# Latent cross attention: keys folded into the ranks of head pairs, scores in two 64-row tiles

## The reference, cut to what matters

```python
q_hk = (hidden_q @ Wq.T).reshape(b, s, H, K)            # H = 16, K = 128
q_big = einsum('bshk,hkq->bshq', q_hk, w_kc_q)          # 384 wide
# layer 2 only: q_big is rotated with sin and cos of the position
kv_rope = kv_c * cos + rotate_half(kv_c) * sin          # (8, 361, 128), shared by all heads
q_r = einsum('bshq,hqr->bhsr', q_big, W_qr)             # 64 ranks per head
k_r = einsum('bld,hdr->bhlr', kv_rope, W_kr)            # 64 ranks per head
scores = einsum('bhsr,bhlr->bhsl', q_r, k_r)
attn = softmax(scores)
ctx_c = einsum('bhsl,bld->bhsd', attn, kv_rope)
ctx_lat = einsum('bhsd,hkd->bshk', ctx_c, w_kc_kv)
out = ctx_lat.reshape(b, s, H * K) @ Wo.T
```

## Time and profile before

| | |
|---|---|
| median of 3 runs | 3009.69 us (3003.22 to 3016.32) |
| profiled execution | span 3002.4 us on the device; its own time is not given beside the span |
| TensorE matmul busy | 2860.6 us, 95% |
| VectorE / ScalarE / GpSimd busy | 1385.1 / 1012.4 / 554.0 us |
| `mscores` matmuls (L1284) | 512 records (2 per fp32 matmul), 166.7 us busy |

### The profile page before, as it was taken

How to read it: one execution, slowest core, us unless ns; L and a number is a source line. 1 busy time by engine, 2 the same in 40 slices (tenths; PEclk the granted TensorE clock), 3 DMA queues, 4 the chain that set the end, 5 groups by cost and what they waited for, 6 DMA issues and landing times.

```text
span 3002.4 us, 37287 instructions
## 1 busy us (share of the span) xinstructions
PE 2860.6 (95%) x14562; PEld 1792.8 (60%) x14562; DVE 1385.1 (46%) x2699; ACT 1012.4 (34%) x2950; POOL 554.0 (18%) x518
## 2 busy tenths in 40 slices
PE   8999988999899999999899899999999988999998
PEld 4555554555666665678655455555554555777767
DVE  4410364511755556611246667676446767111115
ACT  2310172100633334322154222323214473444431
POOL 0000030000110000034112222121000031777750
PEclk9999999999889999999999999999999998999998
DMA  4011102100001110268400000001000102896566
GB/s 176 28 42 49 56 29 84 51 32 0 1 32 67 49 52 29 78 218 297 131 18 24 27 15 35 28 22 60 28 22 29 53 23 73 298 332 203 186 179 156
DMA packets 66675, 249.09 MB, mean 83 GB/s; under 512 B 26554, under 2 KB 28602, under 8 KB 53764
## 3 DMA queue, kind: packets, MB, share of 16 engines
q1 hardware_dynamic: 31776, 177.88, 17.3%
q0 software_dynamic: 31344, 65.30, 6.4%
q10 hardware_dynamic: 3380, 3.53, 0.4%
HBM read 274.53 MB, written 42.13 MB: 105 GB/s over the span
## 4 chain that ended last, share of the span: by engine, by line
PE 80%; DVE 10%; ACT 6%; DMA 2%; issue 1%; POOL 1%; SPq 0%; ACTq 0%; POOLq 0%; DVEq 0%
PE P L1030 32%; PE P L1034 13%; PE P L1416 10%; PE P L1040 4%; PE P L1302 4%; PE P L1284 4%; ACT A L1563 4%; PE P L1059 2%; PE P L1042 1%; DMA A<-outputs 1%; PE P L1275 1%; DVE A L2057 1%; DVE A L2055 1%; DVE A L2056 1%; PE P L1265 1%; PE P L1045 1%
## 5 line engine op out<-in xcount | busy, mean ns | idle before, releaser
L1030 PE MATMUL P<-A,W 128*128 128x400 f32 x1680 | 610.1, 502 | 5.4 <-DVE A L1981 2.9
L1030 PEld LDWEIGHTS P<-A,W 128*128 128x128 f32 x1680 | 317.4, 191 | 245.1 <-issue 7.0
L1476 ACT ACTIVATE A<-P 128x400 f32<-128x400 f32 (+6 forms) x535 | 279.1, 535 | 531.4 <-PE P L1302 170.8
L1030 PE MATMUL P<-X,W 128*128 128x400 f32 x816 | 307.2, 514 | 11.0 <-DMA W<-weights 8.2
L2394 POOL TENSOR_TENSOR A<-A,small 100x1600 f32<-100x1600 f32 x32 | 91.6, 2862 | 1070.1 <-DVE small L1921 1070.1
L2333 DVE TENSOR_TENSOR A<-P,A 128x128 f32<-128x128 f32 (+1 forms) x141 | 44.9, 318 | 457.0 <-ACT A L1729 457.0
L1030 PEld LDWEIGHTS P<-X,W 128*128 128x128 f32 x816 | 155.6, 194 | 130.2 <-issue 17.9
L1563 ACT ACTIVATE A<-A,small 100x100 f32<-100x100 f32 (+1 forms) x640 | 227.5, 366 | 2.2 <-DVE small L1916 2.2
L1040 PE MATMUL P<-C,A 128*128 128x128 f32 (+5 forms) x1511 | 209.8, 261 | 16.7 <-DVE A L1961 5.0
L1040 PEld LDWEIGHTS P<-C,A 128*128 128x128 f32 (+5 forms) x1511 | 168.7, 141 | 65.7 <-issue 38.2
L1034 PE MATMUL P<-A,W 128*128 128x400 f32 x496 | 207.0, 499 | 0.0
(11 more groups left out here) (287 smaller groups left out, 4283.7 us busy)
## 6 DMA issues: line engine op xcount, KB each, us to landing
W<-weights SPq DMA_DIRECT2D x60, 1024.0 KB, 4.8
A<-experts SPq DMA_DIRECT2D x16, 1536.0 KB, 7.7
W<-experts SPq DMA_DIRECT2D x28, 768.0 KB, 5.4
KT<-experts SPq DMA_DIRECT2D x15, 768.0 KB, 6.0
W<-weights SPq DMA_DIRECT2D x17, 640.0 KB, 3.9
A<-experts SPq DMA_DIRECT2D x14, 768.0 KB, 5.6
A<-outputs SPq DMA_DIRECT2D x12, 768.0 KB
W<-outputs SPq DMA_DIRECT2D x8, 768.0 KB
```

The costliest lines, as they stand in the source:

```text
L1030: self.e.matmul(out, a, b, start=i == 0, stop=False)
L1476: self.e.activation(out, in_, ACT.Copy).then_inc(*self.of(*item))
```

## The change

Instead of bringing each query out of its 64 ranks to width 128 (`keyed`), the keys are brought into the ranks. A new step `mkeys` computes, for a group and a batch, the keys of two head pairs: `WK` (128 x 128, the `W_kr` of two heads side by side) times `kf`, 128 x 361 per pair. ScalarE copies them to `KH`, two buffers. `mkeys` of batch t + 1 stands directly behind `mscores` of batch t; the first stands ahead of the loop. `mscores` now multiplies `QR` rows 64a to 64a + 63 with the same rows of `KH`: two heads per pair in two 64-row tiles, and all four banks are taken ahead of the first. `keyed` and `QE` go away, `QR` holds four pairs, and `W_kr` comes by a load of its own per layer (`key_ranks`, 512 KB) instead of with each pair's piece. Some semaphores are shared between kinds of events of the same engine.

```diff
+    def mkeys(self, c, g, b):                              # TensorE
+        self.wait_ge(self.at("key_ranks", c.n))
+        self.wait_ge(self.at("kf", b))
+        for i in range(2):
+            P = self.take(("fold", "kh", c.n, g, b, i), ("kh", c.n, g, b, i))
+            self.e.matmul(P[:, 0:L], c.WK[:, 2 * g + i, :], self.k.kf[:, b, :], start=True,
+                          stop=True).then_inc(*self.of("fold", "kh", c.n, g, b, i))
...
-    def keyed(self, c, p, half):                           # TensorE
-        piece = self.k.load(c.pre, "h", p)
-        P = [self.take(("fold", "qe", c.n, 2 * p + a, half), ("qe", c.n, 2 * p + a, half)) for a in range(2)]
-        self.wait_ge(self.at("qr", c.n, p, half))
-        for a in range(2):
-            rows = slice(64 * a, 64 * a + 64)
-            self.e.matmul(P[a][:, 0:H2], self.k.slot(piece)[rows, 1152:1280], c.QR[rows, p % 2, hs(half)],
-                          start=True, stop=True).then_inc(*self.of("fold", "qe", c.n, 2 * p + a, half))
...
     def mscores(self, c, g, b):
-        for i in range(4):
-            P = self.take(("scores", c.n, g, b, i), ("mexp", c.n, g, b, i))
-            self.wait_ge(self.at("qe", c.n, 4 * g + i, b // 4))
-            self.wait_ge(self.at("kf", b))
-            self.e.matmul(P[0:S, 0:L], c.QE[g % 2][:, i, ss(b)], self.k.kf[:, b, :],
-                          start=True, stop=True).then_inc(*self.of("scores", c.n, g, b, i))
+        P = [self.take(("scores", c.n, g, b, i), ("mexp", c.n, g, b, i)) for i in range(4)]
+        for p in range(2):
+            self.wait_ge(self.at("qr", c.n, 2 * g + p, b // 4))
+            self.wait_ge(self.at("kh", c.n, g, b, p))
+            for a in range(2):
+                rows, i = slice(64 * a, 64 * a + 64), 2 * p + a
+                self.e.matmul(P[i][0:S, 0:L], c.QR[rows, (2 * g + p) % 4, ss(b)], c.KH[rows, b % 2, p, :],
+                              start=True, stop=True).then_inc(*self.of("scores", c.n, g, b, i))
...
+    def mkeys(self, c, g, b):                              # ScalarE
+        self.wait_ge(self.at("x", c.n - 1, 1))
+        if 8 * g + b >= 2:
+            self.wait_ge(self.at("scores", c.n, (8 * g + b - 2) // 8, (b - 2) % 8, 3))
+        for i in range(2):
+            self.wait_ge(self.at("fold", "kh", c.n, g, b, i))
+            self.copy(c.KH[:, b % 2, i, :], self.ps("fold", "kh", c.n, g, b, i)[:, 0:L], "kh", c.n, g, b, i)
...
         yield from (s for s in tail if s)
+        yield "mkeys", c, 0, 0
         for g in range(4):
...
                 if t < NB:
                     yield "mscores", c, g, t
+                if t + 1 < NB:
+                    yield "mkeys", c, g, t + 1
+                elif t == NB and g < 3:
+                    yield "mkeys", c, g + 1, 0
                 yield from steps[n:]
...
-                    more = {1: q[:2], 2: [b[0], q[2]], 3: [b[1], q[3]], 4: [f[0], b[2], k[0], q[4]], 5: [b[3], q[5]],
-                            6: [f[1], b[4], k[1], q[6]], 7: [b[5], q[7]], 8: [f[2], b[6], k[2]], 9: [b[7]]}
+                    more = {1: q[:2], 2: [b[0], q[2]], 3: [b[1], q[3]], 4: [f[0], b[2], q[4]], 5: [b[3], q[5]],
+                            6: [f[1], b[4], q[6]], 7: [b[5], q[7]], 8: [f[2], b[6]], 9: [b[7]]}
...
+            for i, pre in enumerate(("L1_attn_", "L2_attn_")):    # SyncE
+                if p.index >= RING and k.loads[p.index - RING].name == (pre, "o"):
+                    self.wait_ge(self.at(*k.loads[p.index - RING].free))
+                    self.dma("key_ranks", k.subs[4 + 3 * i].WK.rearrange("p h r -> p (h r)"), k.KR[i], "key_ranks", 4 + 3 * i)
             self.piece(p, wd)
```

More of the change, by code:

```diff
@@ L17 @@
 FIRST = 127
+SHARED = {"crossing": "crossed", "up_scale": "scale", "wd_scale": "scale", "weighed": "averaged",
+          "token_of": "list", "tokens": "list", "indices": "list", "ends": "list", "rows": "list",
+          "tiles_of": "places", "end": "places", "slot_of": "places", "ended": "places", "slots": "places"}
 def fm(w):
@@ L769, in plain @@
             first = [(name, c, p) for name in ("mfold", "efold") for p in pairs]
-            query, keyed = ([(name, c, p, half) for half in range(2) for p in pairs] for name in ("query", "keyed"))
-            return first + query[:2] + keyed[:2] + query[2:] + keyed[2:]
+            query = [("query", c, p, half) for half in range(2) for p in pairs]
+            return first + query
         def units(g):
@@ L777, in units @@
             q, b = ([(name, c, 2 * p + a, half) for p, half in pairs for a in range(2)] for name in ("query", "big"))
-            f, k = ([(name, c, p, half) for p, half in pairs] for name in ("fold", "keyed"))
-            return q, b, f, k
+            f = [("fold", c, p, half) for p, half in pairs]
+            return q, b, f
         def back(g, half):
@@ L820, in mla @@
             ahead = plain(0)
-            ahead, left = ahead[:8], ahead[8:]
+            ahead, left = ahead[:6], ahead[6:]
         for step in ahead:
@@ L1229, in mfold @@
         i.then_inc(*self.of("fold", "m", c.n, p))
+        piece.free = "fold", "m", c.n, p
     def efold(self, c, p):
@@ L1627, in fold @@
         self.wait_ge(self.at("fold", "qr", c.n, p, half))
-        self.copy(c.QR[:, p % 2, hs(half)], self.ps("fold", "qr", c.n, p, half)[:, 0:H2], "qr", c.n, p, half)
-    def keyed(self, c, p, half):
-        for h in (2 * p, 2 * p + 1) if c.roped else (2 * p,):
-            self.wait_ge(self.at("fold", "qe", c.n, h, half))
-            self.copy(c.QE[(h // 4) % 2][:, h % 4, hs(half)], self.ps("fold", "qe", c.n, h, half)[:, 0:H2], "qe", c.n, h, half)
+        self.copy(c.QR[:, p % 4, hs(half)], self.ps("fold", "qr", c.n, p, half)[:, 0:H2], "qr", c.n, p, half)
+    def mkeys(self, c, g, b):
[5 more added lines that the diff above has]
+            self.copy(c.KH[:, b % 2, i, :], self.ps("fold", "kh", c.n, g, b, i)[:, 0:L], "kh", c.n, g, b, i)
     def mscores(self, c, g, b):
@@ L2033, in query @@
         self.wait_ge(self.at("fold", "qr", c.n, p, half))
[L2034 to L2042 removed]
+        self.e.tensor_copy(c.QR[:, p % 4, hs(half)], self.ps("fold", "qr", c.n, p, half)[:, 0:H2]).then_inc(*self.of("qr", c.n, p, half))
     def big(self, c, h, half):
```

56 lines of the change are left out of this document (26 added, 30 removed).

## The result

The changed kernel takes 3014.52 us (median of 7 runs, 3011.73 to 3018.44), the kernel before 3005.95 us (7 runs, 3001.51 to 3016.32). The ratio is 1.0027, 95% interval 1.0016 to 1.0037: +8.6 us, under the 0.5% that the prediction called telling. Forecast were 3018 us and +8.4.

The account below looks back on a forecast made before the run. TensorE was taken to bound the kernel (95% busy), in L2 also waiting for VectorE. L1 +1.3, L2 +5.1 and the clock +2 gave +8.4 on the 3002.4 us span; with 7.3 carried over, 3018 us, range 2997 to 3036.

Parts of the forecast that it names:

- The excursion: TensorE's passage into 64-row tiles and back at each scores call: costs 0.40 us whatever it holds.
- Rival C: Scores calls: the pairs of 64-row matmuls don't overlap, +77 us, 3095 us in all; chance 0.03.
- L1: First latent cross attention, plain: TensorE's sum -1.1, first-turn wait +0.5, start wait +1.9, together +1.3 us; clock +2 apart.
- L2: Second latent cross attention, queries rotated on VectorE: +5.1 us, of which 9 us are new waiting for PSUM banks.
- each group of the middle: Two middle groups of L2: step changes from bank waits, added mkeys and lost keyed sum to +2.5 us each.
- last group: Last group of L2: +1.1 us, from four steps of +0.4 and one keyed; mkeys hidden in steps 5 to 7.
- start and group 0: L2's start 0, covered by the 5.06 us rotation wait; group 0 -1.0 us, from two later keyed removed.
- rival D: TensorE's new stops let the granted clock fall, 3.4 to 5.1 us each; 3027 us with two falls; chance 0.21.
- L2's sum on TensorE: TensorE's own steps in L2, without waits: +12.9 for scores and mkeys, -16.8 for keyed, -3.9 us.
- Rival B: Excursion hides and bank waits don't grow: 2979 us, with half the waits 2987 to 2992; chance 0.10 (under -15).
- ScalarE, DMA: ScalarE's new KH copies, assumed 0.50 us each, and the two 512 KB loads are hidden: 0 us.
- The carried 7.3: Whole time: the 7.3 us from profiled span 3002.4 to three-run median 3009.7, carried to the forecast.

Follow-up runs that it names:

- l2_only: Kernel before with the new form in the layer 2 cross attention alone, layer 1 as before: 3113.25 us, ratio 1.0034 to the kernel before.
- kh_early: Changed kernel with KH laid where only the first half of the previous norm must be done: 3109.01 us, ratio 1.0031 to the kernel before.
- l1_only: Kernel before with the new form in the layer 1 cross attention alone, layer 2 as before: 3100.01 us, ratio 0.9999 to the kernel before.
- again: The kernel before, unchanged, timed against itself: 3104.36 against 3104.56 us, ratio 1.0001.
- light_before: Kernel before with one of VectorE's three operations per rotation in L2 left out: 3072.44 us, ratio 0.9902 to the kernel before.
- light_after: Changed kernel with one of VectorE's three operations per rotation in L2 left out: 3072.78 us, ratio 0.9903 to the kernel before.
- trips: Changed kernel with one key matmul put between the two pairs of scores in 56 of 64 calls: 3145.2 us, ratio 1.0140 to the kernel before.
- apart: Changed kernel with both heads of rows 0 to 63 issued before both of rows 64 to 127: 3114.4 us, ratio 1.0035 to the kernel before.

## Why the prediction was right

**The excursion, 0.40 a call.** Right: 0.38. The scores call is 1.39, the keys 1.32, the turn ahead 1.16 instead of 1.06. Rival C (pairs one after another, +77) fell with the first of these.

**L1: predicted +1.3, and +2 for the clock; measured -0.5.** The mechanism held: the wait is for ScalarE's copies behind the norm's second half (L1896), and from the end of the queries ahead (where `keyed` stood before and the mean stands after) to the next query it is 7.25 us (888.21 to 895.46) against 5.60 before (885.70 to 891.30), +1.65 (forecast: +1.8). ScalarE there:

```profile
892.13 0.83 ACT L1492 ACTIVATE A<-P 128x361 f32<-128x361 f32 x2 [1.89 <-DVE X L1896]
```

TensorE's sum is better by 0.6 through 0.38 instead of 0.40, the first turn waits 0.27 instead of 0.5, the start costs 0.2 less, which leaves 0.8 of the difference to the sum that I can't assign. The clock didn't fall:

```profile
885.00:893.00 8.00, 5.51 (x18) 2.94 (x18) 1.82 (x1) 2.97 (x6) 0.00 (x0) 1.00 0.00 0
```

**L2: predicted +5.1, measured +6.6 (+7.5 against the mean of the old stretches).** By its terms:

| term | predicted | measured |
|---|---|---|
| each group of the middle | +2.5 | +2.47, +2.42 |
| `big` directly ahead of the turn, with keyed before | 7.64 | 7.65 |
| last batch of a group, `big` to the query | 0 | 0 (6.23 before, 6.23 after) |
| last group | +1.1 | -0.36 |
| start and group 0 | -1.0 | +2.1 |

The last group was mis-sized. Its last call has no `mkeys` behind it, which I had counted, and the terms as the prediction names them (four times +0.4, less 1.05 for one `keyed`) come to +0.55 and not to +1.1. The chain that covers `mkeys` in steps 5 to 7 is as said, 6.90 us from scores to scores (6.93 before):

```profile
2105.55 1.46 PE L1300 MATMUL P<-A 64*100 64x361 f32 x8
2106.94 1.48 PE L1267 MATMUL P<-KF,A 128*128 128x361 f32 x4
...
2112.45 0.85 PE L1300 MATMUL P<-A 64*100 64x361 f32 x4
```

Group 0 is where the working failed, though the table of stretches seems to say that its start did (+3.1, and -1.0 for the group). The first scores are a poor place for the cut: before, TensorE's long stop of 5.06 us lies behind them, and after, it stops 2.80 us ahead of them. Cut at the `fold` behind the first scores (1682.71 before, 1687.16 after), the start takes 46.83 and 47.12 us, +0.3 where 0 was forecast, and the rest of group 0 takes 127.96 and 129.74, +1.8 where -1.0 was. In that rest the scores of the third batch stand 4.58 us for the rotations, and `fold` later 2.48 us for GpSimd. TensorE there:

```profile
1706.76 2.73 PE L1300 MATMUL P<-A 64*100 64x361 f32 x8 [4.58 <-DVE A L2068]
1709.42 2.27 PE L1267 MATMUL P<-KF,A 128*128 128x361 f32 x4
...
1745.56 3.72 PE L1287 MATMUL P<-A,W 128*64 128x400 f32 x12 [2.48 <-POOL A L2430]
```

Two stretches that begin within these waits, with the granted clock behind the five engines:

```profile
1704.20:1711.02 6.82, 4.26 (x11) 2.15 (x12) 6.66 (x14) 1.07 (x4) 3.08 (x3) 0.50 0.00 0
1745.20:1748.60 3.40, 3.04 (x10) 1.38 (x12) 0.00 (x0) 0.00 (x0) 0.21 (x1) 0.50 0.00 0
```

At 0.50 (1.2 GHz) scores take 2.66 instead of 1.39, `mkeys` 2.11 instead of 1.32, and `fold` 3.65 instead of 2.17: 3.5 us together. That is rival D's mechanism in small, at 2.1 and 1.5 us a fall where it was priced 3.4 to 5.1. In the traces of after, l2_only and kh_early the clock is low for 20.5 us of L2, in those of the old form and order (before, l1_only, again) for 6.8 to 10.2. I had put the +2 for the clock at L1's start, and it came here. That the total came out so near is luck in part: L1 was forecast 3.8 us too high with its share of the clock (+3.3 against -0.5), and L2 1.5 too low.

**L2's sum on TensorE: predicted -3.9 and 9 us of new waiting.** Measured: busy -0.8 with some 3.5 of slow clock in it, idle +7.4. At the full clock throughout and with shorter rotations busy time is 3.8 lower and the changed form is the shorter one (light_before, light_after). Rival B's second condition, that the waits don't grow, fell with this.

**ScalarE, DMA: 0.** Right. The new copy takes 484 ns on average in L1 (0.50 assumed), and after the start of L1 no scores call waits for it:

```profile
L1492 ACT ACTIVATE A<-P 128x361 f32<-128x361 f32 x64 | 27.2, 484 | 3.8 <-DVE X L1896 1.9 <-PE P L1267 1.5
```

**The sum.** +8.4 forecast; the layers measured +6.1 in the profiled pair and +7.0 against the mean, the timed runs +8.6. What of the remaining 1.6 is real can't be told: the interval of the ratio is 4.8 to 11.1 us. The carried 7.3 between profile and median held less well: over seven runs the median of the kernel before is 3005.95, 3.6 above the span of 3002.4 and not 7.3, which is why 3018 became 3014.5 though the difference was right.

## What to carry to other kernels

A step that a neighbour's engine paces doesn't gain from shorter instructions; find the event that releases its buffer and ask whether the change moves it. With buffers going round in a fixed order, count the takes: taking four at once, or slipping one other user between, changes whose release is waited for, and that cost more here than the arithmetic saved. Each passage into half-height tiles and back cost about 0.38 us here, for four records (trips) as for eight, and 0.38 of the 1.21 us that the pairing of four heads saves went to it: gather such matmuls.

## What the runs showed of the hardware

- The order of four 64-row matmuls made no difference: 1.39 us in alternating tiles, 1.40 with both of a tile behind each other (apart).
- A stop of TensorE of 2.49 us at L1's start left the granted clock at 1.00; one of 2.48 us in L2 went with a fall to 0.50, and so did 1.94 us, and 2.85 us at L1's start in apart. The length of the stop alone doesn't tell it.
- The same instructions behind L2 took 960 to 976 us from one execution to the next, and the same kernel timed against itself was good to 0.2%. A difference of 2 us is seen in a trace's stretch, not in the time.
